# Two moves in the emission order: the routing statistics into the token-tile loop, the softmax ahead of the last interleaved units

## What is computed

```python
xn = layernorm(x)
# attention: einsum('blmh,blhd->blhd', att, v) sums the softmax over m, which is 1,
# so only the value projection and the output projection are left
v   = xn @ wv.T + bv
att = v @ w_out.T + b_out
# mixture of 8 experts, the best 2 by router logit, weighted by a softmax over the 2
L   = xn @ router_w.T                     # 2048 x 8
top2_values, top2_idx = top_k(L, 2);  w = softmax(top2_values)
h1  = gelu(xn @ w1[e].T + b1[e])          # 8 experts, 4096 hidden
y_e = h1 @ w2[e].T + b2[e]
out = x + att + sum over the top 2 of w * y_e
```

## Time and profile before

| | |
|---|---|
| time, median of 2 runs | 4006.72 us (4004.52 and 4008.92) |
| the profiled execution: its time | 4006.01 us |
| its span, slowest core (core 5) | 4004.5 us |
| spans of the other cores | 3990.9 to 4002.1 us |
| PE busy | 3759.9 us (94%) |
| ACT, POOL, DVE busy | 621.8, 667.3, 353.7 us |
| chain that ended last | PE 90%, DVE 5%, DMA 2%, ACT 2% |
| mean granted TensorE clock, core 5 | 0.977 |

### The profile page before, as it was taken

How to read it: one execution, slowest core, us unless ns; L and a number is a source line. 1 busy time by engine, 2 the same in 40 slices (tenths; PEclk the granted TensorE clock), 3 DMA queues, 4 the chain that set the end, 5 groups by cost and what they waited for, 6 DMA issues and landing times.

```text
span 4004.5 us, 41928 instructions; the slowest of 8 cores (3990.9 to 4004.5 us)
## 1 busy us (share of the span) xinstructions
PE 3759.9 (94%) x17200; PEld 1681.8 (42%) x17200; DVE 353.7 (9%) x626; ACT 621.8 (16%) x589; POOL 667.3 (17%) x1073
## 2 busy tenths in 40 slices
PE   4877999999999999999999999999999999999994
PEld 2432444444444444444444444444444444444442
DVE  4402100000010000000010100100000010100001
ACT  1420030201102030211203011020302112030210
POOL 1110111111111111111111111111111111111110
PEclk9998999999999999999999999999999999999997
DMA  6651455455545544554557355445445545454544
GB/s 115 109 63 27 71 77 70 76 71 77 76 71 75 75 74 71 76 76 72 76 82 150 45 77 76 72 75 79 69 71 77 76 71 75 73 79 66 78 71 108
DMA packets 255706, 307.08 MB, mean 77 GB/s; under 512 B 51687, under 2 KB 182759, under 8 KB 255520
## 3 DMA queue, kind: packets, MB, share of 16 engines
q0 software_dynamic: 248608, 279.23, 48.6%
q1 hardware_dynamic: 6912, 25.17, 1.9%
HBM read 574.89 MB, written 8.39 MB: 146 GB/s over the span
## 4 chain that ended last, share of the span: by engine, by line
PE 90%; DVE 5%; DMA 2%; ACT 2%; issue 1%; DVEq 0%; SPq 0%; ACTq 0%; POOLq 0%
PE P L447 43%; PE P L367 43%; DVE scr L461 3%; PE P L397 1%; PE P L188 1%; ACT vg L378 1%; DMA x_rot<-x 1%; DMA wvw<-wvf 1%; PE P L258 0%; DVE scr L229 0%; DVE scr L226 0%; DMA scr<-x 0%; DVE x_rot L491 0%; ACT L237 0%; DVEq L46 0%
## 5 line engine op out<-in xcount | busy, mean ns | idle before, releaser
L447 PE MATMUL P<-wvw,vg 128*128 128x512 bf16 x8192 | 1819.9, 383 | 67.2 <-DVE scr L461 50.4
L367 PE MATMUL P<-xnF,wvw 128*128 128x512 bf16 x8192 | 1773.1, 379 | 13.4 <-ACT optF L197 7.1
L447 PEld LDWEIGHTS P<-wvw,vg 128*128 128x128 bf16 x8192 | 804.1, 99 | 1080.7 <-issue 152.6
L367 PEld LDWEIGHTS P<-xnF,wvw 128*128 128x128 bf16 x8192 | 799.4, 98 | 982.6 <-issue 22.5
L378 ACT ACTIVATE vg<-P,b1c_sb 128x1024 bf16<-128x1024 f32 x512 | 570.0, 1113 | 2855.7 <-PE P L367 2854.9
L424 POOL DMA_DIRECT2D wvw<-w2r x512 | 360.1, 706 | 1623.6 <-PE P L447 1550.3
L350 POOL DMA_DIRECT2D wvw<-w1r x512 | 271.5, 533 | 1494.7 <-PE P L367 1491.3
L461 DVE SCALAR_TENSOR_TENSOR scr<-P,wmap_sb,scr 128x512 f32<-128x512 f32 x256 | 192.1, 750 | 3255.9 <-PE P L447 3231.8
L188 PE MATMUL P<-xnF,wvw 128*128 128x512 bf16 x256 | 73.3, 440 | 28.3 <-DMA wvw<-wvf 16.1
L258 PE MATMUL P<-scr 128*128 128x128 f32 x128 | 23.9, 349 | 48.0 <-DVE scr L249 47.7
L397 PE MATMUL P<-wo_sb,optF 128*128 128x512 bf16 x256 | 59.1, 385 | 0.0
(11 more groups left out here) (51 smaller groups left out, 152.6 us busy)
## 6 DMA issues: line engine op xcount, KB each, us to landing
wvw<-w1r POOLq DMA_DIRECT2D x512, 256.0 KB, 4.2
wvw<-w2r POOLq DMA_DIRECT2D x512, 256.0 KB, 4.2
x_rot<-x SPq DMA_DIRECT2D x28, 512.0 KB, 5.0
wvw<-wvf POOLq DMA_DIRECT2D x32, 256.0 KB, 5.0
out<-x_rot SPq DMA_DIRECT2D x16, 512.0 KB, 3.3
scr<-x SPq DMA_DIRECT2D x4, 512.0 KB, 7.8
wo_sb<-wo POOLq DMA_DIRECT2D x8, 256.0 KB, 14.1
b1c_sb<-b1c POOLq DMA_DIRECT2D x1, 128.0 KB, 14.2
```

The costliest lines, as they stand in the source:

```text
L367: pair=pair: t.matmul(pair[:, j * 512:(j + 1) * 512], w1sl[:, sl * 1024 + fc * 128: sl * 1024 + fc * 128 + 128], xnF[:, fc * T + half * 10 ...
L447: t.matmul(W2B[tl], vg[:, f1c * 1024 + tl * 128: f1c * 1024 + (tl + 1) * 128], w2sl[:, sl * 1024 + (f1c % 2) * 512: sl * 1024 + (f1c % 2) ...
```

## The change

`emit_top2_p1(tt)` is issued in `emit_A`, right behind the copy of the logits of the same tile. The ACT Exp and all of `emit_top2_p3` are issued after tile 15 and ahead of the drain loop; `emit_top2_wt` stays behind it. The number of instructions stays the same.

```diff
@@ -279,6 +279,7 @@
         p.wait("vector", "pe", tok)
         tok_Lcopy[tt] = p.do("vector", lambda v, tt=tt: v.tensor_copy(
             wmap_sb[:, tt * E:(tt + 1) * E], logit_ps), inc="dve")
+        tok_p1box[0] = emit_top2_p1(tt)
 
     dcols = scr[:, 2048:2064]
     ecols = scr[:, 2064:2080]
@@ -288,6 +289,8 @@
 
     def top2_m2(tt):
         return scr[:, 2688 + tt * 8: 2696 + tt * 8]
+
+    tok_p1box = [0]
 
     def emit_top2_p1(tt):
         L = wmap_sb[:, tt * E:(tt + 1) * E]
@@ -546,17 +549,14 @@
         if DO_C and tt == 7:
             h1q.extend([(lambda g=g: emit_h1_group(0, 0, g))
                         for g in range(NF1C // 2)])
-    while vpq or h1q:
-        pump()
-    tok_p1 = 0
-    for tt in range(NTT):
-        tok_p1 = emit_top2_p1(tt)
-    p.wait("scalar", "dve", tok_p1)
+    p.wait("scalar", "dve", tok_p1box[0])
     tok_te = p.do("scalar", lambda s: s.activation(ecols, dcols, AF.Exp),
                   inc="act")
     p.wait("vector", "act", tok_te)
     for tt in range(NTT):
         emit_top2_p3(tt)
+    while vpq or h1q:
+        pump()
     for tt in range(NTT):
         emit_top2_wt(tt)
     tok_xnF_all = tok_xnFev[NTT - 1]
```

## The result

The changed kernel is a little slower: the ratio to the kernel before is 1.0023, 95% interval 1.0015 to 1.0031, which is 9 us of 4004. In some runs of every kernel, and in the profile of one experiment, one die ran at a lower clock; times and ratios here are of the others. Its profiled execution took 4012.09 us with a span of 4010.5 us on the slowest core, against 4006.01 and 4004.5 before; its cores end between 3999.6 and 4010.5 us. The forecast was 4012 us, by two moves of 25 to 30 us that cancel, and both are in the trace.

What follows compares the result with a forecast made beforehand. PE, busy 94% of the span, was taken as the bound, with time to be won or lost only where it stands still. 4006.0 - 25.6 (hole) + 28.3 (rounds) + 3.4 (clock) = 4012.1, so 4012 us, range 4002 to 4022.

Steps and rivals of the forecast that it cites:

- two moves of 25 to 30 us that cancel: Whole kernel: 25.6 us gained at the drain's end, 28.3 us lost in loop A; chance 0.66.
- The closed chain: Loop A: logits copy to next logits has no slack, so each tile's round delays the next tile; 28.3 us in all.
- the sum: Terms added up: loop A rounds 28.3 us; whole kernel 4006.0 - 25.6 + 28.3 + 3.4 = 4012.1 us.
- Price of a round: Loop A: six DVE instructions take 1.75 us in tiles 0 to 3, 2.04 beside POOL's weight load in tiles 4 to 15.
- The gain: Drain's end: hole ahead of the output projection shrinks from 33.11 to 7.53 us, gaining 25.6 us.
- The Exp ahead of the drain costs nothing: Drain's start: ACT's Exp and table loads, about 2.8 us, delay no unit; taken as 0, bounds 0 and 2.8 us.
- The clock in tiles 8 to 15: Loop A: longer PE waits slow value units by 1.68 us in two tiles of eight, 3.4 us; bounds 0 and 13.4.
- Hidden rounds: Rival: DVE's slack in loop A swallows the first routing part, leaving only the gain, 3980 us; chance 0.12.
- The clock lost in nearly all tiles: Rival: from tile 8 on the clock falls in nearly all tiles, 4022 us; chance 0.18.
- The hole closed as it should: Against a rival: transposes ahead of the output projection still wait, the 33 us stay, 4034 us; chance 0.04.

Runs made afterwards that it cites:

- fillers in both: Thrown-away PE matmuls added: changed kernel, tiles 4 to 15 (span 3999.8 us); rounds behind normalisation with weight transposes in the drain, tiles 4 to 7 (ratio 0.9888 to before).
- the two-input form: Changed kernel with a round's two tensor_scalar compares written as scalar_tensor_tensor with a tile of ones; ratio 1.0008 to the kernel before.
- the early Exp alone: Kernel before, all rounds still behind tile 15, with Exp and second routing part issued after six drain units; ratio 0.9941 to before.
- the filler: Changed kernel with six thrown-away 128x512 matmuls on PE ahead of the transposes in each of tiles 8 to 15; ratio 1.0001 to before.
- two rounds: Changed kernel with each round of six DVE instructions issued twice; runs of 4051 to 4053 us, ratio 1.0109 to the kernel before.

## Why the prediction was right, and where it was not

*The closed chain.* Right. Where the clock held, a tile is longer by the round of the tile before: from logits to logits tile 9 went from 11.88 to 13.93 us and tile 10 from 10.68 to 12.71, each behind a round of 2.04; and tile 11 went from 11.88 to 13.63 us, behind the one round that took 1.74. With the same rounds behind the normalisation the loop ends at 180.9 us, and with none in the loop at 180.8. With fillers in both, the loop ends at 203.3 with the rounds on the chain and at 176.3 without, 27.0 us apart; the sum had 28.3. That comparison is rough by a microsecond or two, since the one still lost 0.7 us to the clock in tile 13 and the other waited some 0.3 us for DVE's copy in each of tiles 5 to 7.

*Price of a round.* Right but for one tile: 1.75 us in tiles 0 to 3, 2.00 in tiles 4 to 6 and 2.02 to 2.05 behind, beside a weight load. Tile 10's took 1.74 on all cores. In the earlier trace rows POOL's load comes 0.20 us behind the logits of tile 9, and the sum took that for every tile. Behind tile 10's logits the load began only 0.5 us after the copy, before the change (126.16 against 125.62) as after it, and the compare took 0.23 us there. That is 0.3 us of the sum. The Trainium skill (SBUF — State Buffer, Who interferes with whom) gives an exclusive lock on a pair of ports between GpSimd and a VectorE tensor_scalar in its two-port modes; by it a tensor_reduce never contends on trn2, and an instruction with two SBUF inputs contends only with a GpSimd instruction that reads SBUF. The rows agree: beside the load at 117.58 the reduce took 0.16 us and the tensor_scalar 0.52, and the two-input form took 0.23 at the same place.

*The gain.* Right: 25.6 us predicted; 25.7 at the output projection with the early Exp alone, and 27.2 in the changed kernel (between the two moments, 147.25 us before and 120.06 after).

*The Exp ahead of the drain costs nothing.* Right: the value unit at 222.58 had no wait in front.

*The clock in tiles 8 to 15.* Right in kind and near in size: 3.4 us by two tiles of eight at full price; some three of eight lost it, most in part, and the filler gave back 4.3.

*The clock in tiles 4 to 7.* The term that was missing. The sum priced the rounds there and has no term for the clock; the prediction gives no reason for that. On the 8 cores 28 of these 32 tiles lost the clock before the change too, but often only for a part: in 8 of the 32 the transposes still took 1.07 us, after the change in none. The value units behind them grew from 2.5 to 2.9 us to 3.2 to 3.4 in the mean of the cores, and these four tiles are 10.5 us longer in all, where the sum had 1.75 + 2.04 + 2.04 + 0.86 = 6.7. That is 3.8 us too little, of which 0.8 is not the clock but the 1.18 us for which tile 7's unit had waited for its weights: of the 8 cores only three had such a wait, 0.4 us in the mean. Taken together, the clock's part of the loss is some 7.8 us (an estimate: the 12.4 us that fillers gave back with the rounds on the chain, less the 4.6 that they gave back without), where the sum had 3.4.

*The slowest core.* The loop grew by 35.6 us in the mean and not by 31.7. The forecast of 4012 us still fell within 1 us of the profiled execution (4012.09) and of the median of its runs (4012.9), in part by luck. Core 5, on which the sum was made, was among the slow ones before and grew by only 32.9 us, and the 4006.0 us from which the sum starts lie 2 us above the 4004 of the many runs of the kernel before. The ratio over many runs says 9 us, the means at the output projection 8.4, the sum said 6.1.

*The rivals.* Hidden rounds (3980 us) is what the kernel with the rounds behind the normalisation does, so the rival named a true possibility of the schedule, but not of this place. The clock lost in nearly all tiles needed five of eight; it was about three. The hole closed as it should.

## What to carry to other kernels

An engine that is idle for more than half of a stage can still be the bound at one place of it. Before small work is moved into a loop, follow the chain from one iteration to the next, and put the work where this engine waits for the chain and what it does next has slack, not straight behind the instruction that makes the work's input ready. When a queue's stall is removed by an earlier emission, price the place it goes to with the same care as the hole that it leaves: here both were 25 to 35 us.

And a wait of TensorE has a second price, its clock, which is seen in the durations of the matmuls behind it. Price it in every stage that gets longer waits, also in one where the clock falls already: here tiles 4 to 7 paid more of it with one round on the chain than with none. It isn't in proportion to the wait; with two rounds the value units of these tiles took 2.6 to 3.3 us in the mean, no more than with one.

## What the runs showed of the hardware that was not expected

- The longest single wait of PE doesn't say whether the granted clock falls to half. In tile 9 of the changed kernel four cores lost it with no wait in the tile over 1.53 us, as core 6 below (timeline: its value unit takes 3.57 us). In tile 14 two cores kept it behind a wait of 2.12 us, as core 5 below. In the kernel before, with single waits of at most 1.09 us in tiles 8 to 15, it never fell there, and with the six fillers, where waits of up to 1.75 us were left, no value unit of these tiles was slowed on any core.

```profile
125.85 1.06 PE L258 MATMUL P<-scr 128*128 128x128 f32 x8 [1.52 <-DVE scr L249]
128.31 3.57 PE L188 MATMUL P<-xnF,wvw 128*128 128x512 bf16 x8 [1.39 <-ACT vg L381]
```

```profile
197.72 1.06 PE L258 MATMUL P<-scr 128*128 128x128 f32 x8 [2.12 <-DVE scr L249]
199.32 1.89 PE L188 MATMUL P<-xnF,wvw 128*128 128x512 bf16 x8 [0.54 <-ACT vg L381]
```

- 6 thrown-away matmuls of 128x512 (1.46 us) in each of tiles 8 to 15 kept all 64 value units there at full clock and gave back 4.3 us; with 8 to 20 more in tiles 4 to 7 another 8.1 us came back, though 4 of the 64 units in tiles 8 to 15 were slow again.
- A DVE tensor_scalar on 128x8 took 0.52 us in place of 0.23 beside a POOL weight load that began before it, and the scalar_tensor_tensor on the same data 0.23.
